# Writing the squares channel-innermost so that the variance sums read consecutive elements

## The reference, cut to what matters

```python
def layer_norm(x, g, b):
    mu = jnp.mean(x, axis=-1, keepdims=True)
    var = jnp.mean((x - mu) ** 2, axis=-1, keepdims=True)
    return (x - mu) * jax.lax.rsqrt(var + EPS) * g + b

h = layer_norm(x @ fc0_w + fc0_b, ln0_g, ln0_b)
h = jnp.transpose(h, (0, 3, 1, 2))
for i in range(LAYERS):                      # LAYERS = 4
    ...
    x1 = spectral_conv(h, w1, w2)
    x2 = jnp.einsum('bchw,oc->bohw', h, conv_w[i]) + conv_b[i][None, :, None, None]
    h = x1 + x2
    h = jnp.transpose(h, (0, 2, 3, 1))
    h = layer_norm(h, ln_g[i], ln_b[i])
    if i < LAYERS - 1:
        h = gelu(h)
```

## Time and profile before

| what | value |
|---|---|
| median of 3 runs | 4198.41 us (4187.84 to 4206.49) |
| profiled execution, its own time | 4205.0 us |
| its span, first to last instruction | 4203.1 us |
| TensorE busy in the span | 3483.7 us (83%) |
| VectorE busy | 2679.4 us (64%) |
| GpSimd busy | 2530.9 us (60%) |
| ScalarE busy | 2225.5 us (53%) |
| TensorE's mean granted clock | 0.904 of full speed |

### The profile page before, as it was taken

How to read it: one execution, slowest core, us unless ns; L and a number is a source line. 1 busy time by engine, 2 the same in 40 slices (tenths; PEclk the granted TensorE clock), 3 DMA queues, 4 the chain that set the end, 5 groups by cost and what they waited for, 6 DMA issues and landing times. The chain is left out here.

```text
span 4203.1 us, 200921 instructions
## 1 busy us (share of the span) xinstructions
PE 3483.7 (83%) x86496; PEld 2414.4 (57%) x86496; DVE 2679.4 (64%) x3928; ACT 2225.5 (53%) x3724; POOL 2530.9 (60%) x1278
## 2 busy tenths in 40 slices
PE   6778678888678888768888827899999958888988
PEld 4555567777557777657777623344444425555655
DVE  7888467777457777557777612344444447777776
ACT  3444256666346666446666503477777734444444
POOL 8999367777357777446777636544444435555554
PEclk9988889999879999879999857799999979999888
DMA  2222334334333444333443321111111110000000
GB/s 86 93 93 96 101 115 137 137 137 137 111 99 137 137 137 137 113 104 133 136 137 136 123 59 42 46 47 50 50 47 52 41 41 10 11 10 9 10 9 9
DMA packets 171003, 347.88 MB, mean 83 GB/s; under 512 B 53554, under 2 KB 94834, under 8 KB 170562
## 3 DMA queue, kind: packets, MB, share of 16 engines
q1 hardware_dynamic: 167074, 341.32, 25.0%
q0 software_dynamic: 3744, 3.84, 0.6%
HBM read 187.37 MB, written 157.71 MB: 82 GB/s over the span
## 5 line engine op out<-in xcount | busy, mean ns | idle before, releaser
L1195 POOL TENSOR_TENSOR rstd<-var,mhalf 128x16 f32<-128x16 f32 x640 | 1878.0, 2951 | 1202.9 <-DVE var L993 1202.8
L1007 DVE TENSOR_TENSOR zt<-ps,rstd 128x512 f32<-128x512 f32 x640 | 440.8, 689 | 436.6 <-POOL rstd L1195 427.3
L540 PE MATMUL ps<-d,hp 128*32 128x48 f32 x32768 | 508.3, 219 | 172.4 <-ACT hp L747 115.6
L540 PEld LDWEIGHTS ps<-d,hp 128*32 128x32 f32 x32768 | 433.6, 119 | 337.7 <-ACT hp L747 194.5
L993 DVE TENSOR_REDUCE var<-sq 128x16 f32<-128x528 f32 x512 | 534.5, 1045 | 145.0 <-ACT sq L735 143.2
L766 ACT COPY asb<-ps 128x384 f32<-128x384 f32 x512 | 260.0, 508 | 471.6 <-PE ps L540 467.8
L481 PEld LDWEIGHTS ps<-dyi,gt 64*48 64x48 f32 x16384 | 383.3, 175 | 215.9 <-issue 208.2
L481 PE MATMUL ps<-dyi,gt 64*48 64x32 f32 x16384 | 417.1, 251 | 94.2 <-ACT gt L784 70.1
L517 PE MATMUL ps<-ident,hp 128*128 128x128 f32 x2048 | 380.8, 311 | 56.4 <-ACT ho L755 46.8
L1017 DVE TENSOR_TENSOR zt<-zt,gbx 128x512 f32<-128x512 f32 x512 | 373.6, 730 | 12.5
L755 ACT COPY ho<-ps 128x512 f32<-128x512 f32 x512 | 302.0, 590 | 145.8 <-PE ps L517 133.0
(11 more groups left out here) (162 smaller groups left out, 4984.5 us busy)
## 6 DMA issues: line engine op xcount, KB each, us to landing
h_scratch<-ho SPq DMA_DIRECT2D x256, 512.0 KB, 2.8
hc<-h_scratch SPq DMA_DIRECT2D x256, 512.0 KB
wsb<-in_w SPq DMA_DIRECT2D x64, 288.0 KB, 2.9
g_scratch<-gs SPq DMA_DIRECT2D x192, 96.0 KB, 2.3
gt<-g_scratch SPq DMA_DIRECT2D x256, 72.0 KB
tokens<-wsb SPq DMA_DIRECT2D x256, 4.0 KB
xin<-in_x SPq DMA_DIRECT2D x64, 48.0 KB, 1.8
xs<-tokens SPq DMA_DIRECT2D x64, 35.2 KB
```

Source lines behind the costliest of these rows:

```text
L540: last = nc.tensor.matmul(a_ps[row:row + 32, 2 * TRIG * k:2 * TRIG * k + 2 * TRIG], hp[b][:, u, 8 * j + k].rearrange("p v r -> p (v r)"), ...
L1007: nc.vector.tensor_tensor(by_px(zt[h][:, u]), by_px(main_ps(s, h, u)), scale, ALU.mult).then_inc(norm_ready, 1)
L1195: nc.gpsimd.tensor_tensor(rstd[u][:], var[u][:], mhalf[:], ALU.pow).then_inc(rstd_ready, 1)
```

## The change

The squares are stored with the channel innermost: `sq[u]` is 16 rows of 33 and `sql[u]` two blocks of 8 rows of 33. ScalarE reads its PSUM tile in the same order as before and writes each element 33 elements (132 bytes) behind the one before it, in place of consecutive elements. VectorE's sum reads 33 consecutive elements for each pixel, where it read elements 16 (in the last pass 8) apart. Nothing is added or removed: the instructions, their order, their waits and the sizes are the same. The constants in the 33rd place are set once, ahead of the passes.

```diff
-        sq = [sb(f"sq{u}", [128, C + 1, 16]) for u in range(2)]
-        sql = [sb(f"sql{u}", [128, 2, C + 1, 8]) for u in range(2)]
+        sq = [sb(f"sq{u}", [128, 16, C + 1]) for u in range(2)]
+        sql = [sb(f"sql{u}", [128, 2, 8, C + 1]) for u in range(2)]
@@ square
                 if is_last(s):
-                    dst = sql[u][:, :, 0:C, :].rearrange("p v c r -> p v (c r)")
+                    dst, v = sql[u][:, :, :, 0:C].rearrange("p v r c -> p v c r"), 2
                 else:
-                    dst = sq[u][:, 0:C, :].rearrange("p (v c) n -> p v (c n)", v=2)
-                nc.scalar.activation(dst, main_ps(s, h, u).rearrange("p (v n) -> p v n", v=2), ACT.Square
+                    dst, v = sq[u][:, :, 0:C].rearrange("p (v n) c -> p v c n", v=1), 1
+                nc.scalar.activation(dst, main_ps(s, h, u).rearrange("p (v c n) -> p v c n", v=v, c=C), ACT.Square
                                      ).then_inc(sq_ready, 1)
@@ constants
-                nc.vector.memset(sq[u][:, C:C + 1, :], C * EPS).then_inc(consts_ready, 1)
-                nc.vector.memset(sql[u][:, :, C:C + 1, :], C * EPS).then_inc(consts_ready, 1)
+                nc.vector.memset(sq[u][:, :, C:C + 1], C * EPS).then_inc(consts_ready, 1)
+                nc.vector.memset(sql[u][:, :, :, C:C + 1], C * EPS).then_inc(consts_ready, 1)
@@ reduce
                 if is_last(s):
-                    dst, src = var[u][:].rearrange("p (v r) -> p v r", v=2), sql[u][:].rearrange("p v c r -> p v r c")
+                    dst, src = var[u][:].rearrange("p (v r) -> p v r", v=2), sql[u][:]
                 else:
-                    dst, src = var[u][:], sq[u][:].rearrange("p c n -> p n c")
+                    dst, src = var[u][:], sq[u][:]
                 nc.vector.tensor_reduce(dst, src, axis=AX.X, op=ALU.add).then_inc(var_ready, 1)
```

## The result

The changed kernel takes 4450.3 us (median of 6 runs, 4438.4 to 4462.9) against 4195.8 us (median of 6): ratio **1.0605**, 95% interval 1.0579 to 1.0631. It is 255 us slower. The forecast was 4184 us, and the range ended at 4243.

The account below looks back on a forecast made before the run. Bound by a GpSimd-VectorE loop in the stem, a TensorE-ScalarE chain in layer passes, TensorE in the last pass. Stem -16.3, fills -4, squares +5.8 give -14.5 us on 4205.0, scaled to 4184 us; range 4164 to 4243.

Parts of the forecast that it names:

- the price of the square: ScalarE's square, written apart, was taken to grow by 0.03 us, range 0 to 0.41; 192 squares in layer passes, 5.8 us.
- L971 points to zero: VectorE's strided read and write takes 1.011 us against 0.999 for a strided read, suggesting the strided write is free.
- a write of 512 may take up to 1.01 us: Upper bound if VectorE's strided write was hidden behind its read; the 0.597 us square could grow by 0.41 us.
- The rule of the Trainium skill: SBUF access patterns need two hits on a 16-byte line, else a penalty; by it the square costs what the read saves.
- The third case: Layer passes: the write pays as the read did, 0.34 us a square, 65 us lost, 20.3 won; 4243 us, chance 0.25.
- The squares of h = 1 ... 0.03 us hides there: Layer passes: these squares precede a copy TensorE needs only after half of `i1`, so their 0.03 us growth is hidden.
- The sum: VectorE's sum, strided to consecutive reads, goes to 693 ns, saving 0.35 us (512 times) and 0.415 us (128 times).
- Layer passes, steady: nothing: The quicker sum gains nothing in steady layer passes, hidden behind the ScalarE chain with 0.48 us of slack.
- The stem: Loop through GpSimd and VectorE shortens from 6.21 to 5.86 us; 48 waits x 0.34 us, a gain of 16.3 us.
- The fifth case: Stem only half shortens, as another wait takes the place, the first sum waiting for its square; 4192 us, chance 0.09.
- A square that costs nothing: If the strided write is free, the stem, fills and drains gain 20.3 us in all, right at 0.5%.
- 0.34 us more on each would still be hidden: Last pass: both squares run under TensorE's L668 and gelu waits 0.68 us behind them, so 0.34 us more each is hidden.

Follow-up runs that it names:

- experiment 1: Kernel before plus a block timing 512-element ScalarE squares in 18 shapes and VectorE copies in 7; square 0.597 us consecutive, 1.081 us in rows of 33.
- experiment 2: Changed kernel, but ScalarE reads its PSUM tile by pixel and writes 32 squares in a row; ratio 0.9939, 4181.0 us.
- experiment 3: Changed kernel with squares written consecutively (sum alone): 0.9944, 4182.4 us; changed kernel with sums reading elements apart as before (write alone): 1.0613, 4470.5 us.

## Why the prediction was wrong

**The step that failed is the price of the square.** "That row is of the same engine and the same port, and L971 points to zero, so I take 0.03 us": it is 0.553 us. Both rows were read wrongly. L766 writes pairs, and pairs are just the form that costs nothing (0.598 against 0.597 us in experiment 1); to scale "36 ns for 192 jumps" to single elements was to scale the wrong thing. L971 could not tell a free write from a hidden one, which the prediction says and then passes over; experiment 1 shows it hidden. Its bound was the better number: "a write of 512 may take up to 1.01 us" stands beside 1.08 us with nothing else running and 1.15 us in place, so even that bound was low. The rule of the Trainium skill that was cited for the reads holds for these writes as well; the case built on it was given 0.25.

**The third case was the right mechanism, under-sized twice.** The place was right, the squares of h = 0 ahead of L755, L517 and L540, and so was the count of 192. The first size: 0.34 us a square was the cost of VectorE's read; 0.553 gives 106 us in place of 65, and with the clock held up all squares together cost 118. The second: the term for the clock was missing altogether. A longer wait of TensorE was priced at its own length, while behind it the clock fell from 0.97 to 0.83, and the matmuls of L554 went from 0.89 to 1.49 us: 130 us more, about half of the loss. "The squares of h = 1 ... 0.03 us hides there" was not tried at 0.03; at 0.553 they cost 56 us when they alone are long.

**The sum.** Right: 0.693 us predicted, 0.697 measured. "Layer passes, steady: nothing" is right too (1935.9 and 1934.1 us with the quick sum, 1933.0 before).

**The stem.** 16.3 us plus a part of the fills were forecast; the stem ended 9.7 us earlier in experiment 2. The fifth case was at work, in a part of the half steps: the first sum comes to wait 0.2 to 0.4 us for its square in 11 of them, and the short waits of GpSimd that remain are 0.35 us where 0.15 or less was expected. In the changed kernel, with the long square, 6.0 us were left.

**A square that costs nothing** was priced at 20.3 us; experiments 2 and 3 measured 26 and 24 us (0.9939 and 0.9944), within their intervals of it. That is in part luck: the stem gave 9.7 and 8.9 us where 16.3 stood, and the traced last pass became 9.0 and 10.9 us shorter, where at most a fill and a drain of 0.35 us each were forecast. It is the quicker sum that does it, since the kernel before took 1008.1 and, with the block of experiment 1 behind it, 1007.3 us. The traces of experiments 2 and 3 have 0.08 and 0.09 us less in each middle pair, 3 us in all, and most of the rest in the first and the last pairs; why those gain so much is open.

**The last pass.** "0.34 us more on each would still be hidden": that size was not tried, but 0.52 us on each left 0.22 us on a pair, some 7 us over 32 pairs, and nothing that the ratio can tell. Without the quicker sum the same squares cost 29 us there (experiment 3), so the cover was not L668's alone.

## What to carry to other kernels

In these runs a transposition inside an instruction was paid on the SBUF side, at either end, as soon as single elements went 16 bytes or more onwards; put it on the PSUM read, where it was free here, or keep pairs together. Before a row is scaled to a new access pattern, look at whether its runs are of one element. And where TensorE sets the pace, a wait on its chain costs more than its length as soon as the granted clock gives way (here about twice); it is worth looking at the clock of the stretch first, and at whether idle matmuls in the wait bring it back.

## What the runs showed of the hardware that was not expected

- ScalarE, 512 elements of float32: 0.597 us consecutive, 0.620 at a step of 8 bytes, 1.02 to 1.16 at 16 bytes and more, 0.598 with pairs at 64 bytes. Reading PSUM at a step of 64 bytes: 0.597 (VectorE 0.692, against 0.691 consecutive). Reading SBUF so: 1.062.
- The row length matters a little: 1.027 us for rows of 32, 1.081 for 33, 1.161 for 36, 1.065 for 40. In the kernel, beside the other engines, rows of 33 took 1.150 us.
- Ten idle matmuls a pair in the two waits of TensorE took the granted clock from 0.83 to 0.99 and the kernel from 1.0605 to 1.0271 of the time before.
- The clock fell unevenly with the dose: 0.96 to 0.97 without, 0.94 with one long square on the chain in each pair, 0.83 with two. In the kernel of experiment 2, at 0.97, six idle matmuls a pair took the middle pairs of 17.8 and 18.6 us down to the 17.3 of the others.
